# A GpSimd memset and a wait behind each pair of row scatters in the first three parts of an expert dispatch

## What is computed

```
h = layernorm(x) * (1 + cb) + sb                 # second norm, 4096 tokens of 128 floats
probs = softmax(h @ w_router.T)                  # 8 experts
vals, idx = top_k(probs, 2)
gates = sum(one_hot(idx, 8) * vals)
acc  = gelu(h @ Ws1.T + bs1) @ Ws2.T + bs2       # shared expert, all tokens
y[e] = gelu(h @ W1[e].T + b1[e]) @ W2[e].T + b2[e]
out  = x + gb * SCALE * (acc + sum_e gates[e] * y[e])
```

## Time and profile before

| | us |
|---|---|
| median of 3 runs | 707.01 |
| the runs | 700.76, 710.69, 707.01 |
| the profiled execution's own time | 710.08 |
| its span, first to last instruction | 708.0 |
| outside the span | 2.1 |
| mean granted TensorE clock over the span | 0.935 |

### The profile page before, as it was taken

How to read it: one execution, slowest core, us unless ns; L and a number is a source line. 1 busy time by engine, 2 the same in 40 slices (tenths; PEclk the granted TensorE clock), 3 DMA queues, 4 the chain that set the end, 5 groups by cost and what they waited for, 6 DMA issues and landing times. The chain is left out here.

```text
span 708.0 us, 14601 instructions
## 1 busy us (share of the span) xinstructions
PE 605.7 (86%) x4334; PEld 529.2 (75%) x4334; DVE 423.8 (60%) x1745; ACT 331.6 (47%) x1050; POOL 329.4 (47%) x545
## 2 busy tenths in 40 slices
PE   1469999999999999999688434849977999999997
PEld 1249999999999999998456334637856999999983
DVE  2746888888888888888567524442322345454426
ACT  1556666666666666666237313522322344444430
POOL 1025666666666666666111771530355245545430
PEclk9999999999999999999887766869979999999999
DMA  9069900000000000000000125100323567777437
GB/s 206 4 256 413 372 4 1 1 0 0 0 0 0 0 0 0 0 0 2 1 1 4 55 83 180 35 27 1 113 87 106 162 196 228 240 225 237 152 139 240
DMA packets 39667, 66.76 MB, mean 94 GB/s; under 512 B 7394, under 2 KB 26596, under 8 KB 39620
## 3 DMA queue, kind: packets, MB, share of 16 engines
q1 hardware_dynamic: 30948, 54.84, 24.1%
q0 software_dynamic: 4544, 9.45, 3.7%
q10 hardware_dynamic: 4128, 1.91, 1.2%
HBM read 36.25 MB, written 29.92 MB: 93 GB/s over the span
## 5 line engine op out<-in xcount | busy, mean ns | idle before, releaser
L1937 POOL DMA_INDIRECT ys<-yo,dst x78 | 74.7, 958 | 119.4 <-DVE yo L1841 101.6
L1547 ACT ACTIVATE hid<-bank,slab 128x256 f32<-128x256 f32 x156 | 63.8, 471 | 102.8 <-PE bank L1410 79.5
L1929 POOL DMA_INDIRECT xs<-hrow,slot_i x64 | 62.5, 976 | 65.6 <-issue 47.0
L1426 PEld LDWEIGHTS bank<-slab,hid 128*128 128x128 f32 x624 | 77.9, 194 | 7.2 <-issue 5.0
L1426 PE MATMUL bank<-slab,hid 128*128 128x128 f32 x624 | 78.8, 278 | 4.6 <-issue 4.5
L1410 PE MATMUL bank<-hg,slab 128*128 128x256 f32 x312 | 73.7, 380 | 0.4 <-DVE hg L1804 0.4
L1410 PEld LDWEIGHTS bank<-hg,slab 128*128 128x128 f32 x312 | 56.3, 190 | 6.7 <-issue 0.6
L395 PE MATMUL bank<-aH,W2p 128*128 128x128 f32 x192 | 42.2, 302 | 0.1
L395 PE MATMUL bank<-kv,W1b 128*128 128x128 f32 x192 | 41.4, 298 | 0.0
L1836 DVE TENSOR_TENSOR yb<-bank,slab 128x256 f32<-128x256 f32 x39 | 16.5, 424 | 41.3 <-PE bank L1426 37.4
L972 POOL TENSOR_TENSOR nL<-aL,ones 128x128 f32<-128x128 bf16 x32 | 17.7, 553 | 41.9 <-ACT aL L681 41.9
(11 more groups left out here) (338 smaller groups left out, 1908.3 us busy)
## 6 DMA issues: line engine op xcount, KB each, us to landing
slab<-in_slabs_dram SPq DMA_DIRECT2D x39, 578.0 KB, 3.7
xs<-fill SPq DMA_DIRECT2D x34, 528.0 KB, 6.2
xt<-xs SPq DMA_DIRECT2D x39, 132.0 KB
yg<-ys SPq DMA_DIRECT2D x8, 512.0 KB, 6.8
xr<-in_L_attn_x_dram SPq DMA_DIRECT2D x8, 256.0 KB, 9.2
ys<-yo,dst POOLq DMA_INDIRECT x78
xs<-hrow,slot_i POOLq DMA_INDIRECT x64
out_dram<-xr SPq DMA_DIRECT2D x16, 64.0 KB, 1.8
```

Of the source, the lines that this page charges most:

```text
L1426: mm = pe.matmul(y[:, s * D:(s + 1) * D], hid[i % 2][:, n, s * P:(s + 1) * P], right, start=(n == 0 and kind == "expert"), stop=(n == FT - ...
L1547: nc.scalar.activation(hid[i % 2][:, n, :], e_half(i, n), ACT.Gelu_apprx_tanh, bias=bias).then_inc(e_x, 1)
L1929: pool.indirect_dma_start(out=xs[:, :], out_offset=bass.IndirectOffsetOnAxis(ap=slot_i[:, i, c:c + 1], axis=0), in_=hrow[:, c, :], in_offs ...
L1937: pool.indirect_dma_start(out=ys[:, :], out_offset=bass.IndirectOffsetOnAxis(ap=dst[r][:, s:s + 1], axis=0), in_=yo[r][:, s, :], in_offset ...
```

## The change

A tile idle of 1024 floats on each partition is allocated, and a semaphore paused. In dispatch, for the first three parts (k < 3), POOL clears the tile behind each column's pair of scatters and then waits until this memset has ended. c runs from 0 to 23 over the three parts, so there are 24 memsets and 24 waits. Nothing reads idle. The fourth part is as it was.

```diff
             row2 = psb("row2", [P, SUB])
+            idle, paused = psb("idle", [P, 1024]), sem("paused")
             gt = [psb(f"gt{i}", [P, SUB]) for i in range(RX)]
...
                         for i in range(2):
                             pool.indirect_dma_start(out=xs[:, :], out_offset=bass.IndirectOffsetOnAxis(ap=slot_i[:, i, c:c + 1], axis=0),
                                                     in_=hrow[:, c, :], in_offset=None).then_inc(s_half[k // 2], 16)
+                        if k < 3:
+                            nc.gpsimd.memset(idle[:, :], 0.0).then_inc(paused, 1)
+                            pool.wait_ge(paused, c + 1)
```

## The result

| | before | after |
|---|---|---|
| median of 3 runs, us | 707.01 (700.76 to 710.69) | 677.30 (676.28 to 678.36) |
| the profiled execution's own time | 710.08 | 677.3 |
| its span | 708.0 | 675.5 |
| granted clock over the span | 0.935 | 0.957 |

The changed kernel is faster: the ratio is 0.960, with a 95% interval of 0.954 to 0.965, or 29.7 us less by the medians. By the spans of the two profiled executions it is 32.5 us less; nearly all of the difference is the 3.1 us by which the profiled execution of before lay above its median.

A forecast was written before the change was run, and what follows sets the result against it. PE bounds the experts, which start late because long back-to-back POOL scatters hold the other engines. Removing 35.2 us of holds nets 26: 710.1 - 26 = 684 profiled, median 681, 669 to 693 if the mechanism holds, full range 667 to 714.

The forecast's parts named there:

- The holds go with scatters issued back to back: Routing stage: engines stand idle without work (holds) when POOL issues scatters back to back for long, not with scatters as such.
- One scatter in 1.5 us is the drain: POOL's scatters: what fills up drains at about one scatter in 1.5 us; the paced 1.85 lies on the good side.
- The picture behind it: Beside back-to-back scatters: something unknown fills, is full after some 10 us, and empties some 2 us after the last.
- A pair costs 3.7 us (3.48 to 4.17): POOL, parts 0 to 2: two scatters plus memset and gap take 3.7 us, not 2.53, adding 28 us of POOL time.
- 35.2 us go from the routing stage, and the experts start near 462: Routing beside the first three parts: holds of 5.97, 18.9, 1.9 and 8.4 us vanish, sum 35.2; experts start near 462.
- POOL comes late to the fourth part, at 476.1, and PE is then two jobs behind: 9 us given back: Fourth part: first result ready at 469.9, POOL comes at 476.1; PE two jobs (7 us) less far; gain 26 us.
- The fourth part stays with holds, until 508.5: Fourth part: 24 unpaced scatters take 30.3 us, until 506.4, with holds again, ending at 508.5 instead of 541.2.
- Nothing happens: Rival for the whole change: pauses don't touch the holds' cause and added POOL time is covered; 707 us, chance 0.22.
- It gets slower: Rival: holds last while POOL is busy without a break, memsets included; 15.5 us more, 723 us, chance 0.12.
- The gain is given back: Rival: holds go in parts 0 to 2, but POOL's lateness to the fourth part leaves 5 to 12 us; 698 us, chance 0.08.

The follow-up runs named there:

- tiny2: The changed kernel with the memset cut from 1024 floats to 1, the 24 waits kept, on chip 2: 704.22 us, ratio 0.998 to the kernel before.
- latewait2: The changed kernel with two 1024-float tiles cleared in turn, each memset waiting only for the one two pairs before, on chip 2: 676.03 us, ratio 0.957.
- all512: The changed kernel with memsets of 512 floats in all four parts, each waiting only for the one two pairs before, chip 4: 683.55 us, ratio 0.969.
- base2: The kernel before, unchanged, run again on chip 2: 704.18 us, ratio 0.996.
- m256: The changed kernel with memsets of 256 floats instead of 1024, on chip 14, which showed no holds: 659.02 us, ratio 0.998.
- tiny: The changed kernel with the memset cut from 1024 floats to 1, the 24 waits kept, on chip 10, without holds: 657.62 us, ratio 0.998.
- latewait: The changed kernel with two 1024-float tiles cleared in turn, each memset waiting for the one two pairs before, chip 10, without holds: 659.33 us, ratio 1.000.
- m2048: The changed kernel with memsets of 2048 floats instead of 1024 in the first three parts, chip 10, without holds: 680.09 us, ratio 1.033.
- m512: The changed kernel with memsets of 512 floats instead of 1024 in the first three parts, on chip 4: 675.56 us, ratio 0.956.
- all4b: The changed kernel with the 1024-float memset and wait in the fourth part too, on chip 14, without holds: 667.27 us, ratio 1.012.

## Why the prediction was right, step by step

The forecast of 681 us (669 to 693 for its mechanism) met 677.3.

*The holds go with scatters issued back to back.* Right, and shown: tiny2 (waits alone, 704.2) against latewait2 (pause alone, 676.0), both on a chip where before took 707.1.

*One scatter in 1.5 us is the drain.* The estimate was from how long the holds took to begin and end. On chips with holds the experts start at 489.6 to 497.0 for 1.27 us a scatter, 495.1 for 1.31, 471.8 for 1.46, 462.6 for 1.52 and 463.1 to 466.0 for 1.68 to 1.74. So the limit was placed rightly, between 1.46 and 1.52. The picture behind it, something that fills and drains evenly, doesn't fit as well: with a drain of one in 1.5 that is full after 10 us at 1.26, it would take some 70 us to fill at 1.46 (an estimate from these paces), and all512's first hold comes 23 us after its first scatter (409.6 less 386.6). What fills and drains stays open.

*A pair costs 3.7 us (3.48 to 4.17).* It is 3.47, a hundredth under the lower bound. The memset was sized well (0.951 forecast, 0.96 to 0.97 measured). The gap behind its wait is 0.28 us, and the dearer first scatter that the 3.7 allowed for doesn't come: the scatter behind the wait takes 0.97.

*35.2 us go from the routing stage, and the experts start near 462.* They start at 463.44, 33.6 us earlier, of which 0.7 lie ahead of the first scatter. One reading in this sum is off by little: between 410.75 and 432.7 stand ten small operations and not twelve, which is 0.5 us. The holds of this one profiled execution were the right ones to add up, but base2, the same kernel, has 7.4 us less of them ahead of the experts.

*POOL comes late to the fourth part, at 476.1, and PE is then two jobs behind: 9 us given back (35.2 less 26).* This is the term that was mis-sized. Part 2 ended at 470.55 + 0.96 = 471.5 and the first result was ready later, at 472.4, so POOL waited and not PE. The break that was to vanish stayed, 4.01 us for 4.91. 1.1 us was given back, not 9. The step failed twice: in 0.23 us too much for a pair, over 24 pairs, and in the belief that tiles would be ready without a break, though the holds of the fourth part delay the tiles too.

*The fourth part stays with holds, until 508.5.* The last hold ends at 508.34. That the time fits so well is luck: the stretch of scatters began 3.7 us earlier than forecast (472.39 for 476.1) and kept the break of 4.01 us that was to vanish. What was too small is its price: "with no holds in the fourth part either it is 35 and a little more". By the chips without holds all of them cost 48 us, and the fourth part's share is 16 to 18.

*Sum.* -33.6 + 1.1 = -32.5 of span, where -35.2 + 9 = -26 was forecast: the two errors have opposite signs, and the larger is the 9. The forecast's mechanism stands, and its size came out 3.7 us from the median.

*The rivals.* "Nothing happens" is what chips 10 and 14 would show: m256, tiny and latewait lie within 0.2% of before there. But its reason, holds that the pause doesn't touch, is not what happens; there are no holds to touch. On its remark that no row shows what a sequencer fetches during a hold: the DMA view of before does say something. From 462 to 470, while PE, DVE and ACT stand still, it has one queue (packets, MB, share of 16 engines), the scatters' own:

```profile
q0 software_dynamic: 169, 0.34, 12.5%
```

The same view has no line of an instruction queue from 412 to 434 either, and the hold of 420.8 to 432.7 begins and ends in there. So these two holds don't end because instructions arrive. "It gets slower", with a memset as good as a scatter, falls with latewait2. "The gain is given back" by a late POOL is a real mechanism, but it begins beyond 3.5 us a pair: m2048, at 4.32, pays 11.1 us for it, of its 20.8.

## What to carry to other kernels

When all engines but one stand still at the same time with nothing to wait for in the program, look at what the one that works is issuing, and at what pace; here a delay of 0.25 us per indirect scatter was worth 29 us of 705 (m512). Such a delay is free only as long as its engine is still early for its next customer, so work out that moment (here 472 us) before its length is chosen, and take the shortest one that does (512 floats did as well as 1024; 256 was never run where there were holds). And compare a kernel with its predecessor on the same chip: one program took 704 us on one chip and 658 on another.

## What the runs showed of the hardware

*Chips, or their states at the time, differ in the holds and not in the work.* Chips 10 and 14 ran before in 659 to 660 us, chips 2 and 4 in 705 to 707; each was seen at one time only. The same program (tiny and tiny2) had PE busy for 31.45 of 35 us on one and for 10.37 on the other, with scatters 1.31 us apart on both. The scatters' own packets take as long on both, about 0.10 us each: from 387 to 472 they fill 11.4% of the 16 DMA engines' time with 1536 packets in before, and 11.6% with 1594 in tiny. Which resource runs out, and why two of the chips showed no sign of it, no view of the profile names; this is open.

*A memset on POOL blocks some of DVE's operations until it ends.* This was not in the forecast. POOL's timeline of after has this memset:

```profile
396.14 0.97 POOL L1933 MEMSET idle<- 128x1024 f32 x1
```

And DVE's timeline of after, with one operation beside that memset and one without any:

```profile
396.40 0.74 DVE L1710 TENSOR_SCALAR hrow<-rk 128x8 f32<-128x8 f32 x1
...
433.35 0.16 DVE L1710 TENSOR_SCALAR hrow<-rk 128x8 f32<-128x8 f32 x1
```

In m2048, POOL's timeline:

```profile
437.15 1.82 POOL L1933 MEMSET idle<- 128x2048 f32 x1
...
446.30 1.82 POOL L1933 MEMSET idle<- 128x2048 f32 x1
...
450.62 1.82 POOL L1933 MEMSET idle<- 128x2048 f32 x1
```

And DVE's timeline of m2048:

```profile
436.98 2.03 DVE L1710 TENSOR_SCALAR hrow<-rk 128x8 f32<-128x8 f32 x1
...
445.55 2.62 DVE L1762 TENSOR_SCALAR e_i<-etab 128x30 int32<-128x30 f32 x1
...
450.03 2.45 DVE L1776 CAST row_i<-rowf 128x30 int32<-128x30 f32 x1
```

In after the operation of L1710 takes 0.16 us where no memset runs beside it. At 396.40 it lasts until 397.14, and the memset until 397.11. In m2048 the three operations end at 439.01, 448.17 and 452.48, the memsets beside them at 438.97, 448.12 and 452.44. Each ends 0.03 to 0.05 us behind the memset. In m2048 the records of the three start 0.17, 0.75 and 0.59 us before the memset's, while the scatter ahead of it still runs.

The Trainium skill, SBUF — State Buffer, section "SBUF: two separate sides", says that VectorE, for an operation in a 2-port mode, and GpSimd share a pair of ports under an exclusive lock, which whoever starts first keeps for its whole instruction. By that rule a small operation that needs the pair waits for the whole memset, and in that the trace agrees. Whether these operations, TENSOR_SCALAR and CAST, ran in such a mode no view shows, and that the one that starts first wins can't be read from these records, since the three of m2048 start first and still end last.

What it costs is to be seen where PE waits for DVE's ysh, in the last of the router's stages, on the chips without holds. PE's timeline of tiny:

```profile
440.49 1.22 PE L1379 MATMUL bank<-bs2row,ones 1*128 1x256 f32 x2 [4.65 <-DVE ysh L1734]
```

PE's timeline of all4b:

```profile
444.54 1.21 PE L1379 MATMUL bank<-bs2row,ones 1*128 1x256 f32 x2 [6.02 <-DVE ysh L1734]
```

PE's timeline of m2048:

```profile
452.56 1.22 PE L1379 MATMUL bank<-bs2row,ones 1*128 1x256 f32 x2 [8.87 <-DVE ysh L1734]
```

The wait grows from 4.65 us with one float to 6.02 with 1024 (6.6 in latewait) and 8.87 with 2048. For the change as it is that is 1.4 to 2 us here. The experts of all4b start 3.5 us later than those of tiny, but m256, whose memsets are short (0.33 us), starts them at 463.2 as well, so those 3.5 us can't be laid on the lock. With 2048 the start moves by 8.3 us against m256 (471.5 for 463.2), and there the lock is the likely cause; no run took it away by itself. The change as it is meets the lock once more: DVE's two operations that make the first result (L1842) take 1.17 us from 470.50 beside part 2's last memset, which ends at 471.51, and 0.48 us in m512, which has no memset there.
